# Redundant waits removed, setup zero products reshaped, zero products for missing tail steps and two table writes moved in a fused transformer kernel

## Reference

```
x += cross_attention_0(norm(x), context)     # 257 keys, softmax, fp32
x += self_attention_0(norm(x))               # causal, 128-wide head
x += ffn_0(norm(x))                          # 256 -> 1024 -> 256, quantised rows and weights
x += cross_attention_1(norm(x), context)     # 16 heads of width 16, 257 keys
x += local_attention_1(norm(x))              # each token sees 2 neighbours on each side
x += experts_1(norm(x))                      # 8 experts, each token goes to its best 2
```

## Time and profile before

| | us |
|---|---|
| runs of the kernel before | 1423.97, 1426.05, 1428.72 |
| median | 1426.05 |
| the profiled execution, its time | 1423.56 |
| the profiled execution, its span | 1421.7 |

### The profile page before, as it was taken

The page is one execution under the profiler, slowest core; times in us unless marked ns, Lnnn a source line. Parts: engine busy times, 40 slices in busy tenths (PEclk is TensorE's granted clock), DMA queues, the critical chain, the costliest instruction groups (busy, mean ns, idle before and its releaser), DMA issues. The chain is left out here.

```text
span 1421.7 us, 51433 instructions
## 1 busy us (share of the span) xinstructions
PE 1344.6 (95%) x19870; PEld 1133.9 (80%) x19903; DVE 863.1 (61%) x3111; ACT 780.4 (55%) x1855; POOL 647.8 (46%) x1195
## 2 busy tenths in 40 slices
PE   8789999999999988999999978999999999999996
PEld 6467777777777767777777756899999999999995
DVE  5679999999988878899999965333111111111110
ACT  1588888888877777888888865321111111111111
POOL 1234444443454545554555543466544434443442
PEclk9899999999999999999999988999999999999999
DMA  9424444343433333343333314666666666666662
GB/s 328 162 75 117 124 114 125 106 125 105 120 117 93 115 111 98 103 134 105 115 108 106 112 69 149 220 182 186 174 178 178 188 182 180 184 184 184 181 181 56
DMA packets 91179, 201.77 MB, mean 142 GB/s; under 512 B 13568, under 2 KB 48128, under 8 KB 79840
## 3 DMA queue, kind: packets, MB, share of 16 engines
q1 hardware_dynamic: 72304, 176.97, 38.4%
q0 software_dynamic: 15680, 18.69, 7.4%
q10 hardware_dynamic: 2992, 3.28, 0.7%
HBM read 180.88 MB, written 18.29 MB: 140 GB/s over the span
## 5 line engine op out<-in xcount | busy, mean ns | idle before, releaser
L2165 ACT ACTIVATE heT<-ps 128x512 f32<-128x512 f32 x142 | 84.7, 597 | 412.0 <-PE ps L2091 383.5
L2091 PEld LDWEIGHTS ps<-xeT,w_block 128*128 128x128 f32 x2272 | 264.6, 192 | 3.7 <-issue 0.2
L2091 PE MATMUL ps<-xeT,w_block 128*128 128x128 f32 x2272 | 266.1, 275 | 0.0
L2078 PE MATMUL ps<-contexts,heT 128*128 x1136 | 257.5, 379 | 1.6 <-DVE ye L1972 1.6
L1426 ACT ACTIVATE x_prob<-ps,x_nmax 128x257 f32<-128x257 f32 x512 | 210.7, 473 | 67.3 <-DVE x_nmax L1788 64.3
L2078 PEld LDWEIGHTS ps<-contexts,heT 128*128 128x128 f32 x1136 | 210.1, 190 | 27.5 <-issue 2.0
L1788 DVE TENSOR_REDUCE x_nmax<-ps 128x2 f32<-128x514 f32 x256 | 169.2, 682 | 15.8 <-PE ps L1252 14.1
L1260 PE MATMUL ps<-constants,x_prob 128*128 128x128 f32 x1024 | 153.1, 281 | 8.4 <-ACT x_prob L1426 7.2
L1430 ACT ACTIVATE x_probT<-ps 128x512 f32<-128x512 f32 x256 | 147.0, 622 | 10.6 <-PE ps L1260 6.3
L1971 DVE COPY to_ix<-places 128x1 uint32 x71 | 10.9, 154 | 231.5 <-PE ps L2078 223.0
L2206 POOL TENSOR_TENSOR rt_hold<-constants 128x1 f32<-128x1 f32 x143 | 34.4, 240 | 225.3 <-DVE ye L1972 124.2
(11 more groups left out here) (280 smaller groups left out, 2714.4 us busy)
## 6 DMA issues: line engine op xcount, KB each, us to landing
w_block<-in_m_w SPq DMA_DIRECT2D x71, 1024.0 KB
contexts<-in_cn SPq DMA_DIRECT2D x112, 272.0 KB
contexts<-in_cT SPq DMA_DIRECT2D x112, 257.0 KB
contexts<-in_m_w SPq DMA_DIRECT2D x8, 1024.0 KB
contexts<-in_cn SPq DMA_DIRECT2D x4, 1088.0 KB
contexts<-in_lastk SPq DMA_DIRECT2D x32, 136.0 KB
contexts<-in_cT SPq DMA_DIRECT2D x4, 1028.0 KB
xin<-in_x SPq DMA_DIRECT2D x32, 128.0 KB, 2.1
```

Source lines behind the costliest of these rows:

```text
L2078: t = mm(ps[:, 3, 0:D], heT[b][:, k, :], w2[:, e, k, :], start=k == 0, stop=k == FK - 1)
L2091: t = mm(ps[:, half, at:at + P], w1[b][:, k, f * P:(f + 1) * P], xeT[b][:, k, :], start=k == 0, stop=k == H - 1)
L2165: A(heT[b][:, half * FK // 2:(half + 1) * FK // 2, :].rearrange("p k t -> p (k t)"), ps[:, half, :], ACT.Gelu).then_inc(heT_ok.handle, 1)
```

## The change

- `keep_busy` gets a width, and `keep_busy(13)` with 256 columns becomes `keep_busy(60, 55)`: 60 products with 55 columns.
- `q1_norm_T` waits for its PSUM bank only where there is no tile t+2, and then only for the second of the two conditions.
- `values_of` waits for `t1_ok` only for the last unit of the last tile.
- `fill` issues n zero products of 128x128 in place of a step whose tile does not exist, in six places of TensorE's slot, up to slot 31 (two of them up to slot 30); it waits first for the semaphore that says that the bank it writes is free.
- `scatter_behind(s, s + 2, 0)` moves from behind `unit_scaled(s+2, 0)` to the end of GpSimd's slot, past `first_gather(1)`, `q1_rstd`, `c0_rstd`, `ff_rstd` and `unit_last(s+2, 2)`.

```diff
--- before.py
+++ after.py
@@ -1050,9 +1050,9 @@
             mm = nc.tensor.matmul
             tr = nc.tensor.transpose
             pe.wait_ge(zero_ok, 1)
-            def keep_busy(n):
+            def keep_busy(n, width=D):
                 for _ in range(n):
-                    mm(ps[:, 3, 0:D], zero[:, 0:P], zero[:], start=True, stop=True)
+                    mm(ps[:, 3, 0:width], zero[:, 0:P], zero[:, 0:width], start=True, stop=True)
 
             keep_busy(10)
             pe.wait_ge(fold_in, 48)
@@ -1063,7 +1063,7 @@
                 for k in range(H):
                     t = mm(ps[:, 5, h:h + 1], setup_w["x0_Wk_T"][:, k, h * P:(h + 1) * P], cols["x0_bq"][:, k:k + 1], start=k == 0, stop=k == H - 1)
             t.then_inc(su_mm, 1)
-            keep_busy(13)
+            keep_busy(60, 55)
             pe.wait_ge(consts_loaded, 16)
             pe.wait_ge(su_first, FIRST)
 
@@ -1227,7 +1227,8 @@
             def q1_norm_T(t):
                 W(pe, norm_s["query1"], t, "norm")
                 W_counts(t - 2)
-                W_bank(pe, (t + 2, (act_s["cross0"], "probs")), (t - 3, (dve_s["self1"], "x5")))
+                if t + 2 >= tiles:
+                    W_bank(pe, (t - 3, (dve_s["self1"], "x5")))
                 for h in range(H):
                     i = tr(bank(B["q1_norm_T"])[:, h * P:(h + 1) * P], xn["query1"][:, h * P:(h + 1) * P], ident[:])
                 i.then_inc(pe_s["query1"].handle, 1)
@@ -1262,7 +1263,8 @@
 
             def values_of(t, u, b):
 
-                W(pe, t1_ok, t, 2 * u + 2)
+                if t == tiles - 1 and u == NB - 1:
+                    W(pe, t1_ok, t, 2 * u + 2)
                 for r in range(RG):
                     for n in range(KT):
                         for head in range(H * HG):
@@ -1282,6 +1284,13 @@
                     W_bank(pe, (t + 3, (dve_s["cross0"], "x")), (t, (o1_ok, 1)))
                 values_of(t, u, bank(B[f"V{u}"]))
 
+            def fill(s, step, n, b, ok, t, k, last=tiles):
+
+                if step >= tiles and s < last:
+                    W(pe, ok, t, k)
+                    for _ in range(n):
+                        mm(bank(b)[:, 0:P], zero[:, 0:P], zero[:, 0:P], start=True, stop=True)
+
             def slot(s):
                 at(s, unit_probs_T, 1, 1)
                 at(s + 1, ff_hidden_T)
@@ -1289,17 +1298,21 @@
                 at(s + 2, s0_scores)
                 at(s, unit_scores, 2)
                 at(s + 3, c0_scores)
+                fill(s, s + 3, 4, B["c0_scores"], dve_s["self1"], s - 2, "x5")
                 at(s, unit_values, 0)
                 at(s + 1, ff_down)
+                fill(s, s + 1, 4, B["ff_down"], o1_ok, s - 1, 3)
                 at(s, unit_probs_T, 2, 0)
                 route_counts(s - 1)
                 at(s + 3, c0_probs_T)
                 at(s + 2, s0_values)
                 at(s, unit_probs_T, 2, 1)
                 at(s + 2, s0_out)
+                fill(s, s + 2, 3, B["c0_values"], o1_ok, s, 1)
                 at(s, unit_scores, 3)
                 at(s + 1, q1_norm_T)
                 at(s + 3, c0_values)
+                fill(s, s + 3, 4, B["c0_values"], o1_ok, s, 1)
                 at(s, unit_values, 1)
                 at(s + 1, q1_q)
                 at(s - 1, s1_norm_T)
@@ -1321,8 +1334,10 @@
                 at(s + 3, s0_norm_T)
                 at(s + 1, unit_probs_T, 0, 1)
                 at(s + 4, c0_q)
+                fill(s, s + 4, 4, B["c0_q"], o1_ok, s, 3, tiles - 1)
                 at(s + 1, unit_scores, 1)
                 at(s + 3, s0_qkv)
+                fill(s, s + 3, 6, B["s0_qkv"], o1_ok, s, 4, tiles - 1)
                 at(s, s1_out)
                 at(s - 1, s1_values)
                 at(s + 1, unit_probs_T, 1, 0)
@@ -1599,13 +1614,13 @@
                 at(s + 2, unit_last, 1)
                 at(s + 1, s1_rstd)
                 at(s + 2, unit_scaled, 0)
-                scatter_behind(s, s + 2, 0)
                 if s == tiles - 3:
                     first_gather(1)
                 at(s + 3, q1_rstd)
                 at(s + 6, c0_rstd)
                 at(s + 4, ff_rstd)
                 at(s + 2, unit_last, 2)
+                scatter_behind(s, s + 2, 0)
 
             for s in SLOTS:
                 slot(s)
```

## The result

The changed kernel takes 1412.99 us (median of 4 runs, 1407.14 to 1416.28), the kernel before beside it 1427.07 us. The ratio is 0.9899, 95% interval 0.9856 to 0.9942, so 1.0% faster, 14 us. The forecast was 1404, with 1393 to 1417 as its range. The profiled execution is the slowest of the four, 1416.28 us with a span of 1414.5; it is only 7.3 us under the one of before. Of the others one has 1414.2 us of span, and two have 1405.3 and 1408.1 at a higher mean clock. All that follows on single stretches is read from the profiled executions, so it adds up to their 7.3 us and not to the 14 of the medians.

The account below looks back on a forecast made before the run. TensorE, busy 95% of the span, was taken as the bound. From the profiled 1423.56 us, setup +7.4, waits -2, edges -19.5 and tail -7 gave 1402.5, or 1405 on the median; forecast 1404 us, range 1393 to 1417.

Parts of the forecast that it names:

- Edges, -19.5 forecast: Tiles 8 to 19: shifted instruction-packet edges leave the values' run, so waits there go; -19.5 us, bounds -13.4 and -21.
- Setup, +7.4 forecast: Setup filler: 120 narrow rows paced by weight loads at 0.111 us, 13.3 us in all; +7.4 us, bounds +6.3 and +9.6.
- nothing behind absorbs it: After the setup: the first tile is a chain through TensorE, VectorE and ScalarE, so the filler's +7.4 us stays.
- Waits out, -2 forecast: TensorE's slots: 152 already satisfied wait instructions removed, 51 ns each where the queue sets the pace; -2 us, bounds 0 and -5.
- Tail, -7 forecast: Last slots before the experts: moved table writes, fills, clock and shifted stops together; -7 us, bounds -10 and -3.
- the move: Tail, GpSimd: early table writes at the slot's end let the standard deviation come sooner; -4.2 us, bound 0.
- The new stop for tile 30: Tail: the fills put tile 30's packet edge at 222, giving a stop of about 1.2 us.
- the clock, -3: Tail: fills keep TensorE's clock up, winning back a guessed 0.3 of 10 us lost; -3 us.
- Rival 1: Idle time ahead of the values and L765 isn't placed by instruction count and stays; 1422 or 1424.5 us, chance 0.08.
- Rival 2: Slower-walking edge sits on the values' run in nearly all slots, 1.63 us each; 1448 us, chance 0.08.
- rival 3: Setup: narrow products let the clock fall to its lower level, 6 to 12 us longer; 1409 to 1415, chance 0.08.
- Rival 4: Setup: narrow rows run at the pace of their columns, costing nothing; 1397 to 1398 us, chance 0.06.

Follow-up runs that it names:

- run 1: The changed kernel with the setup filler of before (13 products of 256 columns): 1407.91 us, 0.9848 of the kernel before.
- run 12: The changed kernel itself, unaltered, executed once more for a further profile: 1414.06 us.
- run 5: The changed kernel without the 58 zero products of the tail: 1412.07 us, 0.9899 of the kernel before.
- run 10: The changed kernel with 28 narrow setup products instead of 60 and the wait of unit 2's values back in every tile: 1423.89 us.
- run 3: The changed kernel with 28 narrow setup products instead of 60: 1427.59 us, 1.0014 of the kernel before.
- run 4: The kernel before with only the narrow filler (60 products of 55 columns) added: 1431.00 us, 1.0052 of the kernel before.
- run 9: The changed kernel with 28 narrow setup products instead of 60 and the wait of unit 3's values back in every tile: 1421.99 us.
- run 11: The changed kernel with 28 narrow setup products and the waits of units 0 and 1's values and of `q1_norm_T` back in every tile: 1419.56 us.
- run 7: The changed kernel with 60 cheap setup products (32 weight, 17 data columns) and 5 of 256 columns: 1400.15 us, 0.9813 of the kernel before.
- run 8: The version with 60 cheap and 5 wide setup products, without the tail's 58 zero products: 1402.69 us, 0.9838 of the kernel before.
- run 2: The changed kernel with its 60 setup products made 49 cheap ones and 11 of 256 columns: 1409.10 us, 0.9864 of the kernel before.
- run 6: The changed kernel with the early table writes back at their old place in GpSimd's order: 1414.93 us, 0.9891 of the kernel before.

## Why the prediction was right, and where it wasn't

The total came out inside its range, 1412.99 us for 1404, and the mechanism of the largest term was the right one. The other three terms were each too hopeful. In the profiled execution the sum was 1402.5 and the time 1416.28, 13.8 us more: 4.3 in the setup, 2 of the waits, 0.5 of the edges, 7 in the tail. The setup and the tail lie outside their own bounds, and only because the bounds had been added all one way does 1416.28 lie within 1416.8. That part is luck.

**Edges, -19.5 forecast, -19.0 measured** (tiles 8 to 20: 318.13 - 299.16). The largest term, and the one that decided. That idle time with no releaser is a wait for instructions, that it follows the count of instructions, and where the edges would fall, all held: one slot of the twelve kept a stop, of 0.8 us. Three details differ. The walk by 1 or 2 holds for three slots of four; every fourth, with the routing counts in it, moves the edge by 9 or 10 more (from 164 at tile 9 to 153 at tile 10), and the counts of 149 to 170 and 138 to 86 need that. Tiles 8 and 9 of the kernel before are not long (24.81 and 25.17 us as against 24.82 and 25.16), so the loss begins at an edge of 31 there and not at 53. And a unit's values are 32 products, 64 rows, and not the 64 products that the words on the kernel say; the count of 128 rows for two units is right.

The stops cost more than their idle time: 9.3 + 4.1 us stand in the earlier trace rows, 19 came back. Part of the rest is clock, since it is 0.50 for 3.4 us behind the stop of tile 14 and for as long behind the one of tile 16. The windows of the kernel before:

```profile
446.10:449.50 3.40, 3.40 (x28) 2.59 (x27) 1.89 (x7) 0.51 (x3) 2.62 (x5) 0.50 0.86 269
500.70:504.10 3.40, 3.29 (x32) 2.36 (x33) 2.13 (x8) 0.52 (x2) 1.87 (x5) 0.50 0.86 251
```

The Trainium skill, page "Runtime: NRT & Kernel Launch", section "Instruction fetch mechanics", says that instructions come in blocks of 256, which agrees with the walk of the edge in every kernel here. Its "mostly hidden" does not hold where 256 instructions issue in 1.3 us: there a slot was up to 3.7 us longer (28.45 as against 24.74 us, tile 16).

**Setup, +7.4 forecast, +11.7 measured to tile 0.** The filler itself was right: 0.112 us a row for 0.111, and 24.52 - 17.59 = 6.9 at the loop's start, as it could begin 0.5 us sooner. The other 4.8 us lie between there and tile 0 (80.3 us as against 75.5), and they go with TensorE's clock. The windows of the changed kernel, then of the one before:

```profile
48.00:59.00 11.00, 8.62 (x38) 4.36 (x38) 7.91 (x30) 3.44 (x8) 1.80 (x5) 0.53 0.10 30
69.00:86.00 17.00, 13.83 (x75) 8.87 (x74) 12.02 (x30) 9.00 (x18) 6.67 (x13) 0.51 0.05 17
```
```profile
43.00:54.00 11.00, 8.82 (x44) 5.24 (x44) 8.23 (x31) 4.19 (x7) 2.90 (x6) 0.53 0.58 211
```

Both have a stretch near the lower level of 1.2 GHz; the changed one has a second of 17 us, while the pipeline fills and TensorE often idles. The length of the filler doesn't decide it: run 1, with the old one, was near the lower level from 43 to 50, 61 to 71 and 75 to 78 us and reached tile 0 3.6 us after the kernel before, with the same setup work; run 12 had none before 67 us; and run 5, whose setup is that of the changed kernel, reached tile 0 at 101.01 us, 7.9 after the kernel before. From the loop's start to tile 0 it took 73.9 us in run 10, with no stretch at the lower clock, 74.9 in run 3 with one of 3.4 us, and 80.3 in the changed kernel with 27 us of it. So the term had the filler right and left out the clock of the way behind it, which "nothing behind absorbs it" took as fixed. What decides when the clock falls there stays open.

**Waits out, -2 forecast, 0 measured.** Clean slots took 24.70 us before and 24.72 after (tiles 3 to 7). The 51 ns of the earlier trace rows are hidden. The bound of 0 had this case. What the waits do is set how long a slot is in instructions, so the walk, and a stop is longer with them in (runs 3, 4 and 9 to 11).

**Tail, -7 forecast, 0.0 measured.** The parts: the move -5.0 (forecast -4.2); the stop of tile 29 gone as forecast, 1.41 us in the earlier trace rows, of which 0.8 show in its slot where the move is left out (26.07 as against 26.90 us). The new stop for tile 30 was forecast in its place, but at 1.2 us where it took 3.49, since I priced it from a stop with no bulk traffic. That is 2.3 us. The other failed term is the clock, -3: while TensorE stood for 3.49 us the clock fell (0.50 from 852 to 855 us, 0.56 until 858), so that tile 30's slot took 25.94 us where run 7, with no stop, took 19.84. And where no stop is in the way, the fills' own -3 + 1.0 were +0.8 between the profiles of runs 7 and 8 (68.2 and 67.4 us). The one stop cost 6.1 us with what it brought. With the stop out of the way (run 7) the tail came to 70.6 us from tile 28 to the experts, 6.1 under the kernel before and near the forecast's -7, but by another sum: the move and the stop of tile 29 make 5.8 of it, and the fills nothing.

**The rivals.** Rival 1 (stops not placed by the count) fell with runs 2 to 4. Rival 2, the edge on the run in nearly all slots, did not come but was made, in run 3: 14.6 us over the changed kernel, where its price by the rule of 1.63 us a slot (45.5) would be too high; tiles 1 to 28 took 691.2 us as against 670.8, 0.75 us a slot. The changed kernel's profile does not show rival 3, but one execution of run 6, whose setup is the same, does:

```profile
11.12 23.48 PE L1055 MATMUL ps<-zero 128*128 128x55 f32 x120
34.39 0.65 PE L1100 MATMUL ps<-constants,cross_norm 128*128 128x128 f32 x2
```

The clock was 0.50 from 15 to 36 us, a row took 23.27/120 = 0.194 us, and that execution was the slowest of its four at 1426.44 as against 1408.52 to 1415.43. Rival 4 fell: the Trainium skill, page "TensorE: Matmul & The Clock Gate", section "LDWEIGHTS (loading the stationary operand)", gives P / 1.2 ns for a load of P weight columns. An estimate by it is 107 ns for 128 columns, and the filler's 112 agree with it. The 25 ns of the section "Back-to-back issue gap" are, by that section's own words, without the weight load, and no row here reached them beside a load of 128 columns. With 32 weight columns and 17 data columns a row took 3.27/98 = 0.033 us in run 2, near the 27 ns that an estimate by the same formula gives.

```profile
11.09 3.27 PE L1067 MATMUL ps<-zero 128*32 128x17 f32 x98
```

## What to carry to other kernels

Where an engine idles with no releaser at a point that walks through the program from one repetition to the next, count its instructions per repetition: if the rest modulo the packet's size is the walk, the idle time can be moved by padding the program with cheap instructions ahead of the loop, and held off by making the repetition nearly a multiple of the packet. An edit ahead of an unrolled loop, however cheap, can cost or gain a per cent this way (here 1407.91 us with 13 wide products and 1427.59 with 28 narrow ones), so compare slot by slot before crediting the edit itself. Price a stop by what else the DMA queues carry at that moment, and by the clock that it lets fall, not by its own length alone.

## What was not expected of the hardware

- A packet of instructions starts late while bulk DMA is moving: 1.63 us of stop with 0.02 MB moving, 3.49 and 3.55 us with about 1 MB, at the same instruction. The packet's own time was 0.9 to 1.0 us in all three.
- TensorE passed the second edge 1.2 to 1.6 us after the packet of the first had landed, in every slot of every profile with its edge above 211.
- Waits that are long satisfied cost nothing in a clean slot, but a stop is longer with them in: at an edge of 10 to 6 with the waits out a slot was 0 to 0.9 us longer than a clean one, at 12 with them in 1.7 (26.72 and 26.73 us as against 25.00 and 25.01, tiles 13 and 21).
- Two executions of kernels with the same setup can run its 120 narrow rows at 0.112 or at 0.194 us each.
